# One matmul, vector and scalar program for a tokenizer, an attention and a routed feed-forward layer: the second norm's rows split ahead of the heads' output, the logits one unit of matmuls earlier

## What is computed

```python
h = gelu(x[:, 1:] @ W_other + x[:, :1] @ W_read + b)
h = h + attention(layernorm(h))      # softmax over cosine similarities
h = h + ffn(layernorm(h))            # the part that the change touches, below

def ffn(x):                          # 8 experts, model width 256, head width 128
    logits = normed(x) @ normed(sim_matrix) - sigmoid(gates)
    mask = logits > 0                # the best two where none is above 0
    w = softmax(where(mask, relu(logits), -1e9))
    q, k, v = (einsum('tc,ecd,te->td', x, proj, mask) for proj in (q_proj, k_proj, v_proj))
    heads = softmax(causal(q @ k.T / sqrt(128))) @ v
    return einsum('td,edc,te->tc', heads, o_proj, mask * w)
```

## Time and profile before

| | |
|---|---|
| median of 3 runs | 688.79 us (688.14 to 689.27) |
| the profiled execution's own time | 688.87 us |
| its span in the trace | 687.1 us |
| busy: PE, DVE, POOL, ACT | 677.4, 545.5, 407.3, 344.8 us |
| mean granted TensorE clock | 1.00 |

### The profile page before, as it was taken

How to read it: one execution, slowest core, us unless ns; L and a number is a source line. 1 busy time by engine, 2 the same in 40 slices (tenths; PEclk the granted TensorE clock), 3 DMA queues, 4 the chain that set the end, 5 groups by cost and what they waited for, 6 DMA issues and landing times.

```text
span 687.1 us, 17419 instructions
## 1 busy us (share of the span) xinstructions
PE 677.4 (99%) x4856; PEld 434.8 (63%) x4856; DVE 545.5 (79%) x1428; ACT 344.8 (50%) x768; POOL 407.3 (59%) x653
## 2 busy tenths in 40 slices
PE   9999999999999999999999999999999999999998
PEld 8888666565656656565656666565656666565655
DVE  5788977887979787897979788797978788786636
ACT  5977454544546264454546354454536354443444
POOL 7552326675657576665657576565757576562634
PEclk9999999999999999999999999999999999999999
DMA  9581252514323342424324242523324242422121
GB/s 247 146 197 60 62 105 51 120 36 101 75 51 99 56 112 57 106 46 99 69 52 103 50 119 57 102 51 94 70 50 110 52 117 57 101 54 70 23 77 31
DMA packets 128310, 57.29 MB, mean 83 GB/s; under 512 B 100264, under 2 KB 124056, under 8 KB 128152
## 3 DMA queue, kind: packets, MB, share of 16 engines
q1 hardware_dynamic: 127888, 56.60, 36.2%
q10 hardware_dynamic: 392, 0.32, 0.1%
HBM read 30.45 MB, written 9.01 MB: 57 GB/s over the span
## 4 chain that ended last, share of the span: by engine, by line
PE 84%; issue 4%; DVE 3%; DMA 3%; ACT 2%; SPq 1%; POOL 1%; DVEq 0%; ACTq 0%; POOLq 0%
PE bank L1836 69%; PE bank L1756 4%; PE bank L1900 2%; PE bank L1904 2%; PE bank L1902 2%; DMA xT<-xhl 2%; PE bank L1745 1%; DMA pT<-exp_hl 1%; DVE xm L1424 1%; DVE exp_hl L1454 1%; SPq L546 1%; PE bank L1761 1%; PE bank L1913 1%; DVE region_a L1507 1%; DVE exp_hl L1445 1%
## 5 line engine op out<-in xcount | busy, mean ns | idle before, releaser
L1836 PE MATMUL bank<-xm,w_qkv 128*128 128x374 f16 x2304 | 408.6, 322 | 0.0
L1836 PEld LDWEIGHTS bank<-xm,w_qkv 128*128 128x128 f16 x2304 | 221.6, 98 | 148.0 <-DVE xm L1424 3.0
L1047 ACT ACTIVATE region_c<-bank,out_w 128x256 f32<-128x256 f32 x180 | 85.1, 473 | 156.1 <-PE bank L1836 154.9
L1836 PE MATMUL bank<-w_o,aoT 128*128 128x512 f16 x540 | 141.0, 379 | 0.0
L1424 DVE TENSOR_TENSOR xm<-xT,mask_all 128x1496 f16<-128x1496 f16 x128 | 138.9, 1098 | 0.6 <-DMA mask_all<-d_mask 0.3
L1329 DVE SCALAR_TENSOR_TENSOR h<-bank,out_w,h 128x256 f32 (+1 forms) x180 | 86.0, 478 | 62.8 <-ACT region_c L1047 61.2
L756 POOL TENSOR_TENSOR region_c<-region_c 128x512 f32<-128x512 f32 x46 | 69.3, 1508 | 25.3 <-ACT region_c L1047 20.3
L795 POOL TENSOR_TENSOR exp_hl<-exp,exp_hl 128x128 f16<-128x128 f32 (+2 forms) x48 | 51.7, 1079 | 49.2 <-ACT exp_hl L990 47.3
L1836 PEld LDWEIGHTS bank<-w_o,aoT 128*128 128x128 f16 x540 | 51.6, 98 | 44.6 <-DVE h L1329 1.9
L763 POOL TENSOR_TENSOR region_c<-region_c 128x256 f32<-128x256 f32 x46 | 47.9, 1042 | 5.8 <-POOL region_c L756 5.5
L770 POOL TENSOR_TENSOR h<-region_c,h 128x256 f32 (+1 forms) x45 | 41.9, 932 | 15.2 <-POOL region_c L763 14.9
(11 more groups left out here) (213 smaller groups left out, 1018.9 us busy)
## 6 DMA issues: line engine op xcount, KB each, us to landing
mask_all<-d_mask SPq DMA_DIRECT2D x32, 384.0 KB, 4.3
h<-in_x_dram SPq DMA_DIRECT2D x16, 256.0 KB, 4.8
out_dram<-h SPq DMA_DIRECT2D x31, 128.0 KB
rnorm_row<-d_rnorm SPq DMA_DIRECT2D x16, 192.0 KB, 3.9
d_v<-xinT SPq DMA_DIRECT2D x14, 192.0 KB, 4.5
xinT<-d_v SPq DMA_DIRECT2D x56, 48.0 KB, 2.3
h<-in_x_dram SPq DMA_DIRECT2D x15, 112.0 KB, 5.3
out_dram<-h SPq DMA_DIRECT2D x15, 112.0 KB
```

What stands on the lines that cost most here:

```text
L1047: a.activation(prod[:, prod_buf(n, t), q, :], pair_bank(n, p)[:, C:2 * C], ACT.Copy, scale=weights_out(n)[:, t, 2 * q + 1:2 * q + 2]).then ...
L1836: last = t_.matmul(dst, left[lp], right[rp], start=(starts and k == 0), stop=(stops and k == 2), skip_group_check=True)
```

## The change

Three lines change place, and nothing is added or removed. On ScalarE `high_2(f)` goes ahead of the heads' `head_high`, on VectorE `low_2(f)` ahead of the heads' `head_low`, and on TensorE `logits(f)` goes ahead of the unit `M(14)`, right behind `pair(n, 2)`.

```diff
@@ ScalarE, step
+                        if f is not None:
+                            high_2(f)
                         head_high(heads_out(n), probs_bank(n), s_pv_done, n + 1, s_ao_hi,
                                   [(s_pair_done, PAIRS * n)] if later(n) else [], heads_scale)
-                        if f is not None:
-                            high_2(f)
@@ VectorE, step
                     output_weights(n)
+                    low_2(f)
                     head_low(heads_out(n), probs_bank(n), s_ao_hi, n + 1, s_ao_lo, 1.0 / (P_SCALE * Q_SCALE))
-                    low_2(f)
                     head_low(qT, qkv_bank[0], s_q_hi, m + 1, s_q_lo, qkv_out)
@@ TensorE, step
                     pair(n, 2)
+                    logits(f)
                     M(14)
-                    logits(f)
                     pair(n, 3)
```

## The result

| | before | after |
|---|---|---|
| median of 8 runs each | 688.61 us (688.14 to 690.28) | 691.39 us (690.33 to 692.07) |
| span of the profiled execution | 687.1 us | 688.9 us |
| ratio of the runs | | 1.0035 (95%: 1.0024 to 1.0046) |

The change makes the kernel slower by some 2.4 us (0.35% of 688.61; by the interval 1.7 to 3.2). The ratios in this document weigh all runs and are not the quotients of the medians, which lie 2.8 us apart here. The prediction, 689.2 us in a range of 687.4 to 690.8, had the trade of two waits right and one of them too small.

What follows compares the result with a forecast made beforehand. TensorE, busy 99% of the span, was taken as the bound. A new 0.26 us wait less the old 0.20 us in 11 steps, less 0.24 us won in steps 1, 2 and 14, gave +0.4 us: 689.2 us, range 687.4 to 690.8.

Steps and rivals of the forecast that it cites:

- the trade of two waits: Likeliest case: the logits' wait goes, a new wait at `pair(n, 0)` replaces it, +0.06 us a step; chance 0.67.
- TensorE sets the pace, and only its waits count: Whole kernel: PE is busy 99% of the span, so only waits of TensorE can be won or cost time.
- The old wait, 0.20 us in twelve steps: At the logits, TensorE waits for the DMA to land `xT`: 0.20 us a step in twelve steps, to be won.
- The logits could start at 312.23, and slide to 312.25: Step 6: transposes allow logits at 312.23, 0.93 us earlier; their place on TensorE slides from 311.99 to 312.25, so no wait.
- The heads' low half 0.69 us later, `pair(n, 0)` 0.26 us late: Step 6: `head_low` behind `low_2` ends at 309.31, so `pair(n, 0)` starts at 309.36 instead of 309.10.
- Step 2 has no new wait: Step 2: rows are ready 2.07 us before `head_high`, so nothing is put off and the old 0.20 us is won.
- The sum: All steps: 11 x 0.06 - 0.20 - 2 x 0.02 = +0.4 us, median after 689.2 us.
- a weight load laid bare: Rival at `pair(n, 0)`: the stall also pays the 98 ns load, 1.5 us slower, 690.3 us; chance 0.14.
- Its point of decision, a wait of 0.35 us: At `pair(n, 0)`: a wait of 0.35 us or more makes the loss distinguishable from no change.
- The transposes did come earlier: Rival at the logits: queue or DMA engines hold the transposes until 313.11, 11 us slower, 700 us; chance 0.04.
- slower `mask_tokens`: Rival: VectorE meets GpSimd elsewhere, one `mask_tokens` takes 1.60 us for 1.07 in 12 steps, 6.4 us, 695; chance 0.05.
- The range: Median after between 687.4 and 690.8 us: the likeliest case, uncertain by 0.08 us a step, and the bare load, 0.81.

Runs made afterwards that it cites:

- The two edits to the waits: Whole change, plus `low_2` waiting for the old transposes before the rows, and `pair(n, 0)` waiting for the heads' low half alone: 688.61 us, ratio 0.9998.
- The turned order of waits: Whole change, but in `low_2` the wait for the old transposes stands ahead of that for the rows' high part: 689.54 us, ratio 1.0010.

## Why the prediction was wrong

- *TensorE sets the pace, and only its waits count.* Right: the two waits account for the periods in the table above.
- *The old wait, 0.20 us in twelve steps.* Right: ScalarE's edit alone takes it away, and the period falls by 0.21 us.
- *The logits could start at 312.23, and slide to 312.25.* Right in kind: they wait no more. In step 6 the low transpose was issued from 309.78 on and landed 2.78 us later, at 312.56, and the logits started at 312.79, while a landing that TensorE waited for stood 0.05 us before the logits (313.96 and 314.01, in the chain without VectorE's edit). So there were some 0.2 us to spare, because the slide was larger.
- *The heads' low half 0.69 us later, `pair(n, 0)` 0.26 us late.* **This is the step that failed.** The mechanism was right, its size was not: 0.41 us, past the 0.4 us that the prediction named as a sign of being wrong. Of the 0.15 us, 0.07 is the release of `low_2` (0.20 for the 0.13 taken from the earlier trace rows) and 0.10 the release of the pair (0.15 for the 0.05 taken from the earlier trace rows); rounding and a quicker start of `high_2` (0.03 for 0.05) give the rest back. The prediction held that every part had a row of the same instruction at the same size. The first row was of `low_2` itself, but with one wait fewer: the edit puts `out_w_ready` in front of it, as the order of VectorE's list shows. The second was of another matmul (L1900), with a single wait in front of it, where `pair(n, 0)` has two. The two edits to the waits took off 0.09 us each, and 0.18 together.
- *Step 2 has no new wait.* Wrong. Its early rows came from the 1.02 us that TensorE had waited in that execution. After, step 2 is 0.42 us late like the others, so there are twelve such steps and not eleven.
- *The sum.* +0.06 us in 11 steps and -0.24 was +0.4. With what was measured it is 12 x (0.41 - 0.20) = +2.5 us, and the runs show +2.4.
- *The rivals.* The nearest in time, a weight load laid bare (690.3 us), had the right place and almost the right price, 0.10 us, for a wrong reason. Its point of decision, a wait of 0.35 us, was the one that was passed. The 107 ns that the Trainium skill gives for a load (TensorE: Matmul & The Clock Gate, LDWEIGHTS) did not show at `pair(n, 0)`: with one wait fewer the pair started 0.06 us after its operand was written, load and all. The transposes did come earlier, as the logits do not wait. Of slower `mask_tokens` the trace shows no sign: 21 of the 128 instructions at L1424 take over 1.3 us, for 20 before.
- *The range* gave 0.08 us a step for a sum of seven pieces, where two pieces had no row with the same waits. They alone made 0.17 us.

## What to carry to other kernels

Where two results leave one engine close together, the one with the least time to spare goes first, and the other's start can be moved alone: here the first of three edits wins 0.4% by itself, and the two that were to complete it lose more than that. What an engine needs between a release and its work is a price of that instruction in that place, not of the engine pair: count its waits, those that an edit moves in front of it too, and the values worked out between them, and put the wait that comes last last. And before a step of a trace is taken as a kind of its own, look for a wait in it that may belong to that one execution.

## What the runs showed that was not expected

One sequencer instruction more in front of the work, if it is worked off after the release, cost some 0.07 to 0.09 us: VectorE needed 0.20 us with two of them, 0.13 with the `ALU_OP` alone and 0.11 with the `EVENT_SEMAPHORE` alone; TensorE needed 0.15 us with one and 0.06 with none. When every step is on the edge, each is 1 us of 689 by the waits (12 x 0.09). The turned order of waits is not better everywhere: in steps 1 and 14, where the other wait is another one, `low_2` followed `high_2` by 0.14 to 0.15 us with it and by 0.10 without.

In step 2 a transpose takes longer in some executions and not in others: `pT<-exp_hl` 4.62 us in the first trace of the kernel before (2.90 us is usual for the last one of such a pair), and `xT<-xhl` (2.77 us is usual) 3.73 us in the second trace of it, 3.81 us without VectorE's edit, and longest in the kernel with VectorE's waits turned round:

```profile
154.59 4.43 DMA xT<-xhl
```

There the logits of step 2 were 1.56 us late. What holds these transfers was not looked into.
